# lora_a in one load, taps issued by ScalarE, the fourth x step behind the first gathers, tap copies ahead of the first gates

## The reference, cut to what matters

```python
# layer 1
out = lax.conv_general_dilated(x, weight, window_strides=(1,), padding=[(4, 4)], feature_group_count=4)
out = out + einsum('nd,od->no', c, c_weight)[:, :, None] + bias[None, :, None]
h = relu(layernorm(xf @ gw1.T + gb1) * gamma + beta)
gates = h @ gw2.T + gb2                     # top 2 of 8, softmax, capacity
main = xf @ weight.T
tmp = einsum('ni,eir->enr', xf, lora_A) * w.T[:, :, None]
out = main + einsum('enr,ero->no', tmp, lora_B) * ALPHA
# whole
x = x + L0_ffn(L0_cond(x, cond_128, ...), ...)
x = x + L1_ffn(L1_cond(x, cond_128, ...), ...)
```

## Time and profile before

| what | before |
|---|---|
| timed runs, median | 304.42 us |
| profiled execution, its own time | 302.07 us |
| its span | 300.3 us |
| granted TensorE clock, mean | 0.997 |
| TensorE busy | 288.7 us (96%) |
| VectorE, ScalarE, GpSimd busy | 195.4, 125.3, 95.1 us |
| moved by DMA | 52.75 MB |

### The profile page before, as it was taken

The page is one execution under the profiler, slowest core; times in us unless marked ns, Lnnn a source line. Parts: engine busy times, 40 slices in busy tenths (PEclk is TensorE's granted clock), DMA queues, the critical chain, the costliest instruction groups (busy, mean ns, idle before and its releaser), DMA issues.

```text
span 300.3 us, 6135 instructions
## 1 busy us (share of the span) xinstructions
PE 288.7 (96%) x1982; PEld 236.5 (79%) x1982; DVE 195.4 (65%) x506; ACT 125.3 (42%) x263; POOL 95.1 (32%) x124
## 2 busy tenths in 40 slices
PE   7999979999999999999999999999999999999994
PEld 5788957687978797879877987798777876777883
DVE  1655964743669466946594749474948555899885
ACT  3325834434622572258224822392237326103430
POOL 4361425123311431143114311431113235217660
PEclk9999999999999999999999999999999999999998
DMA  5796699893869487946794669458646790005887
GB/s 142 186 339 143 154 252 233 212 213 75 220 185 210 87 218 211 178 93 181 228 189 104 161 224 207 104 154 204 129 104 163 187 206 6 0 2 188 320 331 280
DMA packets 74400, 52.75 MB, mean 176 GB/s; under 512 B 44405, under 2 KB 61477, under 8 KB 74377
## 3 DMA queue, kind: packets, MB, share of 16 engines
q1 hardware_dynamic: 72936, 51.37, 69.1%
q10 hardware_dynamic: 1120, 1.07, 1.1%
q0 software_dynamic: 320, 0.02, 0.2%
HBM read 35.67 MB, written 16.78 MB: 175 GB/s over the span
## 4 chain that ended last, share of the span: by engine, by line
PE 54%; DMA 14%; SPq 12%; DVE 8%; issue 5%; ACT 4%; POOL 1%; DVEq 0%; ACTq 0%
PE ps_g L1139 10%; PE ps_d L1139 9%; DMA xg<-x1d 8%; PE ps_c L1277 7%; DMA x1d<-xq 7%; PE ps_a L1100 5%; PE ps_t L1293 3%; SPq L353 3%; PE ps_a L1089 3%; SPq L356 2%; ACT xq L632 2%; PE ps_d L1318 2%; PE ps_d L1319 2%; PE ps_d L1500 1%; PE ps_d L1505 1%
## 5 line engine op out<-in xcount | busy, mean ns | idle before, releaser
L512 POOL TENSOR_TENSOR o1l<-o,o1h 128x512 fp32r<-128x512 f32 x30 | 39.4, 1313 | 150.2 <-ACT o L644 150.2
L1139 PE MATMUL ps_d<-wt_hi,o1h 128*128 128x336 f32 (+1 forms) x120 | 41.1, 342 | 0.3 <-DVE y_all L961 0.3
L1139 PE MATMUL ps_d<-wt_hi,o1l 128*128 128x336 f32 (+1 forms) x120 | 38.7, 323 | 0.0
L1139 PE MATMUL ps_d<-wt_lo,o1h 128*128 128x336 f32 (+1 forms) x120 | 38.6, 322 | 0.0
L1277 PE MATMUL ps_c<-xg,cw 96*32 96x512 f32 x256 | 34.1, 604 | 3.1 <-DMA xg<-x1d 3.1
L955 DVE TENSOR_TENSOR oT<-ps_c,biasT 128x512 f32<-128x512 f32 x32 | 21.9, 686 | 22.8 <-PE ps_c L1277 21.9
L1139 PE MATMUL ps_g<-wt_hi,o1h 128*128 128x336 f32 x112 | 35.6, 318 | 0.6 <-ACT tmp_all L659 0.4
L1139 PE MATMUL ps_g<-wt_hi,o1l 128*128 128x336 f32 x112 | 35.5, 317 | 0.0
L1139 PE MATMUL ps_g<-wt_lo,o1h 128*128 128x336 f32 x112 | 35.4, 316 | 0.0
L632 ACT ACTIVATE xq<-y_all 128x512 f32 (+1 forms) x29 | 31.9, 1152 | 7.3 <-DMA x1d<-xq 4.1
L1100 PEld LDWEIGHTS ps_a<-pm,xT 128*128 128x128 f32 x256 | 30.2, 192 | 1.4 <-issue 0.8
(11 more groups left out here) (258 smaller groups left out, 577.7 us busy)
## 6 DMA issues: line engine op xcount, KB each, us to landing
xg<-x1d SPq DMA_DIRECT2D x64, 254.0 KB, 5.1
xg<-x1d SPq DMA_DIRECT2D x32, 256.0 KB, 3.8
x1d<-xq SPq DMA_DIRECT2D x30, 256.0 KB, 3.6
xs<-in_x_dram SPq DMA_DIRECT2D x6, 1024.0 KB, 6.2
out_dram<-xT SPq DMA_DIRECT2D x16, 256.0 KB, 2.1
out_dram<-xg SPq DMA_DIRECT2D x15, 256.0 KB, 2.1
y_all<-in_x_dram ACTq DMA_DIRECT2D x2, 512.0 KB, 5.2
y_all<-in_x_dram SPq DMA_DIRECT2D x1, 1024.0 KB, 5.7
```

Source lines behind the costliest of these rows:

```text
L512: pool.tensor_tensor(lo, o1[t % 2][:, :, :], hi.bitcast(fp32), ALU.subtract).then_inc(s_o1l, 1)
L1139: last = T.matmul(bank[:, 0:columns], a[:, Q - 1 - q, :], w[:, q, first:first + columns], start=(q == 0 and n == 0), stop=(q == Q - 1 and ...
```

## The change

lora_a is loaded by one DMA whose runs are 64 numbers (4 rows of 16), which takes another order of `ga`: blocks of 16 columns outermost, then the phase q, then the 16 columns. Router part, ScalarE's and GpSimd's copies into `wt_hi` and `wt_lo`, and the operand of line 1306 follow that order. The four tap DMAs go from SyncE's list to ScalarE's, between `x_transposed(0)` and `u_out(0)`. The load of x's fourth step goes from the set-up to SyncE's step 0, behind the gather of tile 1. VectorE's tap copies, with their waits, go from behind the mixture copies to between `rs` and `gates0(0)`.

```diff
@@ -29,6 +29,7 @@
     ER1 = E1 * R1
     G1 = gw1.shape[0]
     GC = G1 + ER1
+    GB = G1 // R1
     MC = (H + GC) // 2
     TAPS = convw.shape[2]
     CG = convw.shape[1]
@@ -63,6 +64,9 @@
             shape = list(v.shape)
             shape[axis] = n
             return v.broadcast_to(shape)
+
+        def blocks(v):
+            return v.rearrange("p q (e r) -> p e q r", r=R1)
 
         def wait(eng, s, value):
 
@@ -92,7 +96,7 @@
         rs = sb("rs", [P, UC])
         b_hi = sb("b_hi", [P, H], fp32r)
         b_lo = sb("b_lo", [P, H], fp32r)
-        ga = sb("ga", [P, Q, GC])
+        ga = sb("ga", [P, GC // R1, Q, R1])
         cw = sb("cw", [P, G, Q, CG])
         gw2bd = sb("gw2bd", [P, NT, E1])
         ident = sb("ident", [P, P])
@@ -346,15 +350,9 @@
             sp.dma_start(wn, wmain.rearrange("(c p) h -> p c h", p=P)).then_inc(s_ld["w"], 16)
             sp.dma_start(gw1n, gw1).then_inc(s_ld["gate"], 16)
             sp.dma_start(gw2n, row(gw2, 1, NT)).then_inc(s_ld["gate"], 16)
-            for i in range(2):
-                sp.dma_start(xs[i][:, :, :], x_v[2 + i]).then_inc(s_x[i], 16)
-            sp.wait_ge(s_zero, 1)
-            for i in range(Q):
-                sp.dma_start(taps[i:C:Q, :, 7 - i:7 - i + TAPS],
-                             convw.rearrange("o c k -> c o k")).then_inc(s_ld["conv"], 16)
-            for e in range(E1):
-                sp.dma_start(ga[:, :, G1 + e * R1:G1 + (e + 1) * R1],
-                             lora_a[e].rearrange("(m q) r -> m q r", q=Q)).then_inc(s_ld["lora_a"], 16)
+            sp.dma_start(xs[0][:, :, :], x_v[2]).then_inc(s_x[0], 16)
+            sp.dma_start(ga[:, GB:, :, :].rearrange("p e q r -> p e (q r)"),
+                         lora_a.rearrange("e (m q) r -> m e (q r)", q=Q)).then_inc(s_ld["lora_a"], 16)
 
             def write(u, t):
 
@@ -387,6 +385,7 @@
                     write(s, 3)
                     sp.wait_ge(s_x1w[1], 16)
                     gather(s, 1)
+                    sp.dma_start(xs[1][:, :, :], x_v[3]).then_inc(s_x[1], 16)
                     sp.wait_ge(s_x1w[2], 32)
                 else:
                     write(s, 0)
@@ -520,8 +519,8 @@
                     mixing(1)
                     pool.wait_ge(s_gah, 1)
                     pool.wait_ge(s_gm, 2)
-                    pool.tensor_tensor(wt_lo[:, :, H:H + GC], ga[:, :, :], wt_hi[:, :, H:H + GC].bitcast(fp32),
-                                       ALU.subtract).then_inc(s_gal, 1)
+                    pool.tensor_tensor(blocks(wt_lo[:, :, H:H + GC]), ga[:, :, :, :],
+                                       blocks(wt_hi[:, :, H:H + GC].bitcast(fp32)), ALU.subtract).then_inc(s_gal, 1)
                     o1_low(0, 0)
                     return
                 if has(s, 2):
@@ -598,6 +597,10 @@
             act.wait_ge(s_attd, 1)
             nc.scalar.activation(atte, att, ACT.Exp).then_inc(s_atte, 1)
             x_transposed(0)
+            act.wait_ge(s_zero, 1)
+            for i in range(Q):
+                act.dma_start(taps[i:C:Q, :, 7 - i:7 - i + TAPS],
+                              convw.rearrange("o c k -> c o k")).then_inc(s_ld["conv"], 16)
             u_out(0)
             act.wait_ge(s_sp["bias"], 1)
             nc.scalar.activation(biasT[:, :], ps_t[:, 0:NB], ACT.Copy).then_inc(s_ss["bias"], 1)
@@ -705,8 +708,8 @@
                     gate0_exp(1)
 
                     act.wait_ge(s_ss["gw1"], 1)
-                    act.wait_ge(s_ld["lora_a"], 16 * E1)
-                    nc.scalar.activation(wt_hi[:, :, H:H + GC], ga[:, :, :], ACT.Copy).then_inc(s_gah, 1)
+                    act.wait_ge(s_ld["lora_a"], 16)
+                    nc.scalar.activation(blocks(wt_hi[:, :, H:H + GC]), ga[:, :, :, :], ACT.Copy).then_inc(s_gah, 1)
                     gm_out(1)
                     u_out(2)
                     o_hi(0, 0)
@@ -862,6 +865,12 @@
                                      ps_v[C * r:C * r + C, 128:128 + NB].rearrange("p (n r) -> p n r", r=BT)[:, :, r])
             last.then_inc(s_mbsb, 1)
             V.tensor_copy(rs[:, :], ps_v[:, RS0:RS0 + UC]).then_inc(s_ss["rs"], 1)
+            dve.wait_ge(s_ld["conv"], 16 * Q)
+            dve.wait_ge(s_zero, 3)
+            for r in range(3):
+                last = V.tensor_copy(cw[C * r:C * r + C], taps[:, :, Q * r + 4:Q * r + 4 + Q]
+                                     .rearrange("p (g o) q -> p g q o", o=CG))
+            last.then_inc(s_cw, 1)
             gates0(0)
             dve.wait_ge(s_ld["rows"], 16 * 2)
             def y_out(u, t):
@@ -970,17 +979,11 @@
                     for t in range(NT):
                         V.tensor_copy(gw2bd[G1 * t:G1 * t + G1, t, :],
                                       ps_v[G1 * t:G1 * t + G1, Q * G1:Q * G1 + E1])
-                    V.tensor_copy(ga[:, :, 0:G1], ps_v[:, 0:Q * G1].rearrange("p (q g) -> p q g", q=Q))\
+                    V.tensor_copy(ga[:, 0:GB, :, :], ps_v[:, 0:Q * G1].rearrange("p (q e r) -> p e q r", q=Q, r=R1))\
                      .then_inc(s_ss["gw1"], 1)
                     for j in (1, 3):
                         dve.wait_ge(s_mps, 2)
                         V.tensor_copy(mix_home(2, j), mix_part(j)).then_inc(s_msd, 1)
-                    dve.wait_ge(s_ld["conv"], 16 * Q)
-                    dve.wait_ge(s_zero, 3)
-                    for r in range(3):
-                        last = V.tensor_copy(cw[C * r:C * r + C], taps[:, :, Q * r + 4:Q * r + 4 + Q]
-                                             .rearrange("p (g o) q -> p g q o", o=CG))
-                    last.then_inc(s_cw, 1)
                     w_lo(0)
                     w_lo(1)
                     gates0(1)
@@ -1304,7 +1307,7 @@
                     wait(pe, s_y, s * NT)
                     for q in range(Q):
                         last = T.matmul(ps_g[:, 0:GC], o1[t % 2][:, Q - 1 - q, :],
-                                        ga[:, q, :], start=(q == 0), stop=(q == Q - 1))
+                                        ga[:, :, q, :], start=(q == 0), stop=(q == Q - 1))
                     last.then_inc(s_gp, 1)
 
                 def delta(u, t):
```

## The result

The changed kernel takes 312.19 us (median of 4 runs, 311.98 to 312.25), the kernel before beside it 304.25 us (303.94 to 304.55). The ratio is 1.029 (95% interval 1.023 to 1.034): slower, by 7.9 us of the medians. The profiled executions stand 10.1 us apart: 312.14 us (span 310.4) against 302.07 us (span 300.3). The difference has a reason that matters for the case: TensorE's clock falls in some executions of the kernel before and not in others, and the medians of those two kinds stand some 4 to 5.5 us apart (experiment 5); the profiled one kept its clock, and the three that made the 304.42 us, which were not traced, stand where the others do. In the experiments a ratio is taken against the executions of before within 1.5% of its fastest, nearly all of which kept it.

A forecast was written before the change was run, and what follows sets the result against it. TensorE was taken as the bound, busy 288.7 of 300.3 us. Gates +3.8 and queue with x load -0.2 gave +3.6 us, added to the earlier median of 304.42 us: 308.0 us, range 302.2 to 309.4 us.

The forecast's parts named there:

- Parts 1 and 5: SyncE's freed queue: first x1 write 3.16 us earlier, 1.97 us wait before first convolution gone; lora_a's layout costs zero.
- Part 2: Four tap DMA issues on ScalarE: 0.77 us each, 3.07 us, in an idle stretch, so nothing waits.
- part 3: VectorE's tap copies ahead of the first gates: waiting for the tap DMAs delays the chain by 3.8 us.
- T: Time at which the last tap DMA lands, forecast at 23.5 us, behind the large loads.
- S: Shift of the chain behind VectorE's early tap wait: landing plus copies minus 20.23 us and slack; forecast 3.8 us.
- slack: Margin of 0.26 us between gms ending on VectorE (24.54 us) and TensorE needing it (24.80 us).
- the mixing-weight row: Profile row: mixing-weight DMAs issued 3.13 to 6.20 us held GpSimd until 9.81 us; read as waiting behind another queue's load.
- C: Rival: DMA queues take turns, taps land at 20.1 us, +0.2 us, 304.6 us; chance 0.10. Over half the engines, 24 to 25 us.
- rival F: Taps later still, ScalarE held in its issues, or TensorE's clock falling in the gap: 309.5 us and above; chance 0.07.
- Part 4: x's fourth-step load among the gathers: costs 3.0 us in a full DMA stretch, leaving 0.2 us of the 3.16 us gain.
- the gates: Sum's term for tap copies ahead of VectorE's first gates: +3.8 us.
- queue and load: Sum's term for SyncE's freed queue together with x's moved load: -0.2 us.

The follow-up runs named there:

- experiment 5: Kernel before, unchanged, profiled in an execution with the lower clock: 304.43 us; with five pairs of dummy matmuls ahead of the first convolution: 301.72 us.
- experiment 4: Kernel before with only lora_a's single load and its layout: 299.63 us; with only the taps issued by ScalarE: 300.44 us.
- experiment 1: Changed kernel with tap copies at their old place: 302.70 us; with x's fourth-step load back in the set-up as well: 300.26 us.
- experiment 3: Changed kernel with taps issued early by GpSimd: 303.54 us; with x's third step and lora_a held back until the taps landed: 304.81 us.

## Why the prediction was wrong

conv(s,t) is the convolution of tile t of step s: conv(0,0) is the first of all, conv(1,0) the first of the next step.

**Parts 1 and 5, SyncE's queue and lora_a: right.** conv(0,0) has no wait. lora_a's layout cost nothing: line 1309 has 297/299/374 ns, the same as before. One load took SyncE 0.57 us here and 2.38 us in experiment 4.

**Part 2, ScalarE's issues: the wrong end.** I took 0.77 us each, 3.07 us; it was 6.04 us here, 5.16 to 7.92 in the other profiled executions. "ScalarE's queue has nothing in it" was no reason: the engine is held all the same, while other queues are full. In the change it was hidden by part 3, as said; alone (experiment 4) it made TensorE wait nearly 1 us.

**Part 3, the landing T: the step that failed first.** The form of the sum held: S = T + copies - 20.23 - slack, with copies at 0.79 us (0.75 forecast), gives 26.07 + 0.79 - 20.23 - 0.26 = 6.4 us, and the transposes came 6.37 us later (so close by luck in part: the slack of 0.26 us belongs to gms; v came 6.69 us later, and this path had 0.32). T was wrong: 26.07 us for 23.5. The end of the load was forecast well, 22.1 us, when all but 36 of its 2 KB runs had gone by 22. Mis-sized is what I put behind it, 1.0 us for the taps' own runs and 0.4 us to land: it was 3.3 us, to about 25.3, and 0.8 us.

The mechanism was wrong with it. I let the taps stand behind the whole load, by the mixing-weight row. They stand behind nothing and take turns instead, about one large run for each tap run, so that 408 of 1,056 packets had gone by 22 us; and behind the load the rest still had a partner to take turns with, lora_a's 1,024 short runs, which the change had put there and I had left out. How much of the 3.3 us is lora_a's no run shows by itself.

I had the rule of turns among the rivals (C), with its working over half the engines giving "24 to 25 us", and counted it with the forecast without letting it move the number. The mixing-weight row could not decide: those DMAs are small runs beside a large load too, and turns could make them just as late. I read a row that both rules explain as evidence for one.

The waiter was also another than named. I had v and the router behind it, to TensorE's lines 1248 and 1337. First came ScalarE's exponential of the gates, with the third tile's copy queued behind it. The delay is the same, but TensorE stops sooner and all at once, in one gap of 6.1 us.

**The term that was missing: the clock, 3.7 us.** The forecast has a gap of nearly 4 us in it and prices only the gap. I wrote the clock into rival F, "falling in the new gap", at 0.07 with the rest of F. Even a gap of 2 us in the kernel before makes it fall in about half the executions (19 of 35 and 9 of 23), and a gap of 6 us left a mean clock of 0.972 to 0.983 in all eight that were seen. All rows of before showed 1.00; the median's 2.35 us above the profiled execution was the hint that I passed over. The Trainium skill (TensorE: Matmul & The Clock Gate, HAM oscillation) warns of waits for DMA that slow the clock for the work behind them; windows of this case show it.

**Part 4, x's load: right in the profile.** 3.16 - 3.0 was to leave 0.2 us of the gain; of the 2.0 us won at conv(0,0), 1.7 were gone again at conv(1,0), and experiment 1 prices the load's place at 2.4 us. The DMA share of 1.17 in 43 to 61 us agrees with the reason given. By the medians it does not come out so well: the kernel with the copies back, which has the freed queue and the moved load, stands at 1.008 of the executions of before that kept their clock, 2.4 us above them and not 0.2 below. The profiled execution of before was itself no typical one of these: its 302.07 us is as long as their longest (302.02 us beside experiment 4, median 300.06), so what it shows as a wait to be won may not be there in the others.

By the sum: +3.8 for the gates was +6.4, -0.2 for queue and load was about -0.3, the clock's +3.7 was not there, and 0.3 us came in the rest. +3.6 became +10.1 in the profile. By the medians it is 7.9 us: the executions behind the median of before, by experiment 5, hold a fall of the clock of their own.

**Which parts are worth having.** The steps in one line, medians (not all measured side by side): lora_a in one load alone 299.63 us; with the taps on ScalarE 300.26 us; with x's load behind the gathers 302.70 us; with the copies ahead of the gates 312.19 us. The first is faster than both kernels. Against the executions of before that kept the clock it gains little (0.995, 0.991 to 0.999), against the median of all 35 it gains 4.5 us: its chief gain is that the clock no longer falls. Why a wait of 2 us, gone, gives only 0.4 us against the median of those that kept the clock stays open; timed executions leave no trace. The copies' move by itself, without the other parts, was not tried.

## What to carry to other kernels

A wait for a DMA put ahead of the critical chain costs its landing minus the deadline, and the landing of many short runs beside a large load on another queue goes by count: so many runs per engine, times one large run, for as long as the large load lasts, and then times one run of whatever follows it there. Its own queue and its few bytes do not help; issuing it ahead of the large load, or needing it later, does. Price a new gap in TensorE as the gap plus the slow work behind it, and when a kernel's executions fall in two kinds, look for the wait that halves the clock: removing 2 us of waiting may be worth 4. A load taken from an idle stretch into a full burst cost 2.4 us or more here for 3.0 us of transfer, in both places of the burst that were tried.

## What the runs showed of the hardware that I had not expected

- Two queues on the same engines alternate run by run: 46 to 46 packets in one microsecond. Beside that, 262 short runs took three microseconds beside large ones and 569 one microsecond without.
- Four DMA issues of short runs held ScalarE for 5.16 to 7.92 us and SyncE for 10.1 and 10.23 us. The stop goes with the place, not with the load: lora_a's eight issues took 7.64 us behind the taps and 16.44 us where the taps had been.
- Waits of 2.12 and 2.27 us were followed by a granted clock of 0.50; behind the second the next step stands 3.1 us later. A wait of 1.97 us was not, in the profiled execution of before. With the wait of before filled with idle matmuls the clock stayed at 1.00.
- A 16 KB packet of instruction fetch took 0.9 us (changed kernel, 1.9% of 16 engines in 3 us) and 1.1 us (experiment 3). In both kernels the last tap runs came a microsecond or more behind the rest; that the fetch caused it is not shown.
